# Three read-backs of expert gates move from the sync queue to GpSimd's queue

## What is computed

```python
def _L1_ffn_ref(x, router_w, router_b, expert_w, expert_b):
    scores = jnp.einsum('bsh,eh->bse', x, router_w) + router_b
    probs = jax.nn.softmax(scores, axis=-1)
    top_probs, expert_ids = jax.lax.top_k(probs, K)
    y = jnp.einsum('bsh,edh->bsed', x, expert_w) + expert_b
    out_k = jnp.take_along_axis(y, expert_ids[..., None], axis=2)
    w = top_probs / (jnp.sum(top_probs, axis=-1, keepdims=True) + 1e-09)
    out = jnp.einsum('bsk,bskh->bsh', w, out_k)
    return out
```

## Time and profile before

| what | value |
|---|---|
| median of 3 runs | 945.74 us (945.5 to 946.44) |
| the profiled execution | 946.11 us |
| its span, from the first to the last instruction | 944.3 us |
| busy in the span: PE, DVE, ACT, POOL | 741.0, 576.6, 404.1, 386.8 us |

### The profile page before, as it was taken

How to read it: one execution, slowest core, us unless ns; L and a number is a source line. 1 busy time by engine, 2 the same in 40 slices (tenths; PEclk the granted TensorE clock), 3 DMA queues, 4 the chain that set the end, 5 groups by cost and what they waited for, 6 DMA issues and landing times. The chain is left out here.

```text
span 944.3 us, 11558 instructions
## 1 busy us (share of the span) xinstructions
PE 741.0 (78%) x3622; PEld 585.7 (62%) x3622; DVE 576.6 (61%) x994; ACT 404.1 (43%) x875; POOL 386.8 (41%) x305
## 2 busy tenths in 40 slices
PE   7877888685547869877999677888886997787688
PEld 5645656454327869877898545666664775565455
DVE  4167779679765532312111387899796859777835
ACT  1549275374233324422245373644724455355120
POOL 1045745655672411303003144654366433653430
PEclk9899999798677989999999888888977999899899
DMA  9469755355494658888677597787679565967600
GB/s 353 128 205 343 228 154 152 91 136 142 127 266 113 185 170 242 254 258 232 191 241 223 152 233 190 195 220 189 158 201 252 151 168 143 268 167 187 195 1 21
DMA packets 84067, 177.66 MB, mean 188 GB/s; under 512 B 12671, under 2 KB 32357, under 8 KB 83365
## 3 DMA queue, kind: packets, MB, share of 16 engines
q1 hardware_dynamic: 79172, 169.67, 63.6%
q0 software_dynamic: 4832, 7.24, 2.6%
HBM read 156.15 MB, written 20.69 MB: 187 GB/s over the span
## 5 line engine op out<-in xcount | busy, mean ns | idle before, releaser
L1759 PE MATMUL PS<-PR,CM 128*128 128x304 f32 (+1 forms) x672 | 186.8, 420 | 92.3 <-POOL PR L806 63.2
L806 POOL TENSOR_TENSOR PR<-ST,V 128x608 f32<-128x608 f32 x96 | 142.4, 1483 | 185.5 <-DVE ST L1340 153.8
L1759 PEld LDWEIGHTS PS<-PR,CM 128*128 128x128 f32 x672 | 126.8, 221 | 134.7 <-POOL PR L806 76.8
L976 ACT ACTIVATE dA<-dA,negA 128x304 f32<-128x304 f32 x192 | 93.7, 540 | 151.3 <-DMA BB<-rows_d 151.1
L1340 DVE TENSOR_TENSOR_SCAN ST<-dA,PS 128x608 f32<-128x608 f32 x96 | 136.4, 1420 | 15.1 <-ACT dA L976 11.0
L1028 ACT ACTIVATE HID<-PS,WX 128x128 f32<-128x128 f32 x204 | 59.6, 367 | 150.0 <-PE PS L1759 149.9
L719 POOL TENSOR_TENSOR dA<-dA,aP 128x607 f32<-128x607 f32 x48 | 70.7, 1474 | 71.5 <-ACT aP L996 69.7
L1536 DVE TENSOR_TENSOR xp<-PS,WXB 128x192 f32<-128x192 f32 x34 | 12.2, 358 | 127.0 <-PE PS L1759 127.0
L1329 DVE TENSOR_TENSOR PS<-BB,PS 128x608 f32<-128x608 f32 x96 | 76.2, 794 | 21.5 <-DMA BB<-rows_d 10.7
L1759 PE MATMUL PS<-XT,WX 128*128 128x128 f32 x408 | 83.3, 288 | 1.0 <-ACT HID L1028 1.0
L1759 PE MATMUL PS<-XT,WXR 128*128 128x128 f32 x408 | 83.0, 287 | 0.0
(11 more groups left out here) (380 smaller groups left out, 1318.6 us busy)
## 6 DMA issues: line engine op xcount, KB each, us to landing
dA<-rows_d SPq DMA_DIRECT2D x144, 304.0 KB, 4.4
BB<-rows_d SPq DMA_DIRECT2D x144, 304.0 KB, 5.1
WX<-ex_m SPq DMA_DIRECT2D x34, 576.0 KB, 4.0
WX<-ex_m SPq DMA_DIRECT2D x34, 387.0 KB, 3.8
slots_d<-WXR SPq DMA_DIRECT2D x8, 960.0 KB, 8.8
WXR<-ex_r SPq DMA_DIRECT2D x34, 192.0 KB, 4.9
CM<-c SPq DMA_DIRECT2D x1, 4430.0 KB, 19.6
WX<-gates_d SPq DMA_DIRECT2D x3, 1216.0 KB, 6.6
```

The source lines that it names most:

```text
L806: nc.gpsimd.tensor_tensor(PRq[:, c % 2], STq[:, c % 2], DIRS[k].Cw.unsqueeze(1).broadcast_to([128, QB, T]), ALU.mult).then_inc(q_product.s ...
L976: last = nc.scalar.activation(dAq[:, slot, i, :], dAq[:, slot, i, :], ACT.Exp, scale=negA[:, j:j + 1])
L1759: return nc.tensor.matmul(out, lhsT, rhs, start=first, stop=last)
```

## The change

The body of `read_gates` is the same, but it stands on POOL's queue instead of SP's. In `part_b`, POOL calls it ahead of its eleventh product (n = 10). `write_gates` stays on SP.

```diff
@@ SP
-            def read_gates(g):
-
-                sp.wait_ge(gates_out.sem, gates_out.after(g, 16))
-                sp.dma_start(GX[:, 0:EXPERTS, :].rearrange("p e t -> p (e t)"),
-                             gates_d.rearrange("e t -> (e t)").unsqueeze(0).broadcast_to([128, EXPERTS * T])).then_inc(gates_in.sem, 16)
-                for h in range(2):
-                    every = gates_d.rearrange("(e h) t -> h e t", h=2)[h:h + 1, :, :]
-                    sp.dma_start(GX[h * DR:(h + 1) * DR, EXPERTS:, :], every.broadcast_to([DR, EXPERTS // 2, T])).then_inc(gates_in.sem, 16)
...
                 if g + 1 < GROUPS:
                     write_rows(g + 1, 0)
-                if g:
-                    read_gates(g - 1)
             store(GROUPS - 2)
@@ POOL
+            def read_gates(g):
+
+                pool.wait_ge(gates_out.sem, gates_out.after(g, 16))
+                pool.dma_start(GX[:, 0:EXPERTS, :].rearrange("p e t -> p (e t)"),
+                             gates_d.rearrange("e t -> (e t)").unsqueeze(0).broadcast_to([128, EXPERTS * T])).then_inc(gates_in.sem, 16)
+                for h in range(2):
+                    every = gates_d.rearrange("(e h) t -> h e t", h=2)[h:h + 1, :, :]
+                    pool.dma_start(GX[h * DR:(h + 1) * DR, EXPERTS:, :], every.broadcast_to([DR, EXPERTS // 2, T])).then_inc(gates_in.sem, 16)
...
             def part_b(g, tail, nxt):
                 far = after_next(nxt)
                 for n in range(QSTEPS):
+                    if g is not None and tail is not None and n == 10:
+                        read_gates(tail)
                     if g is not None:
                         product_step(g, 1, n)
```

## The result

The changed kernel takes 958.88 us (median of 4 runs, 955.56 to 960.67) where the kernel before took 945.7 us beside it: 13.2 us between the medians. The ratio of runs taken side by side is 1.0106, 95% interval 1.0073 to 1.0140, so 10 us slower (7 to 13). The forecast was 950.1 us, its range ended at 953.0.

What follows compares the result with a forecast made beforehand. No engine holds the span; the last-ending waits at the three gate reads count, with DMA engines full at the seams. 946.11 + 1.8 (end) + 2.6 (seams) = 950.5, or 950.1 us on the median's scale; range 944.8 to 953.0.

Steps and rivals of the forecast that it cites:

- The last read: End of program: POOL issues the gate read 1.6 us later than SP, first byte 0.2 us later; +1.8 us.
- the two delayed products: End: POOL's last two products, delayed up to 3.5 us by the three issues, finish before the first mixture piece.
- The late start of the seams: Both seams: row reads wait for the last row write to land, so the first transfer comes 1.3 us later.
- If the DMA engines do the same 11.6 us of work from a start 1.3 us later, the last of what PE needs lands 1.3 us later: Both seams: full engines move 3040 KB at an unchanged rate; +1.3 us at each, +2.6 us.
- The slow clock behind a waiting PE: Seams: idle PE restarts at the 1.2 GHz level; only a rival counted it, up to 2.5 us of work lost.
- the rival with a cold PE: Seams: all four slots get ahead of the gates, and PE's slow stretch begins later; 951.3 us, chance 0.15.
- PE needs all 3040 KB before it can run on: Seams: PE's step 1 order needs the gates (1824 KB) and two row slots (608 KB each).
- Gates last: Seams: four slots get ahead, gates in at 819.7 us at the second; 5.6 us in all, 951.3 us, chance 0.15.
- the 0.4 us for landing: Second seam, gates-last case: added to the transfers' end at 819.3 us, putting the gates at 819.7 us.
- The seams cancel: Seams: engines alternate between queues, second slot 1 us earlier, gates 0.9 us late; seams cost about 0; 947.5 us, chance 0.20.
- The marks: Signs for right: DVE's first seam wait gone or short, a later wait instead; POOL's last pieces at about 899.3 us.
- The mark against it: Seams: DMA windows well over 269 GB/s would make the forecast fall, since it rests on full engines.

Runs made afterwards that it cites:

- The second set: The changed kernel itself, timed again beside the kernel before: ratio 1.0083 (1.0050 to 1.0117), or 7.9 us slower.
- e1: Kernel before with only the last gate read on POOL's queue (n = 10), the seams still on SP: ratio 1.0046 (1.0016 to 1.0075).
- e5: Kernel before with the seam gate reads on ACT's queue, behind POOL's tenth backward product; last read on SP: ratio 1.0025 (0.9998 to 1.0053).
- e11: Changed kernel with ACT's output instructions ahead of the exponentials of steps 2 to 4: ratio 1.0123 (1.0085 to 1.0161).
- e6: Kernel before, but at the seams SP issues the gate reads behind the second slot's row reads: ratio 1.0053 (1.0023 to 1.0083).
- e2: Kernel before with only the seam gate reads on POOL's queue (n = 10), the last read on SP: ratio 1.0066 (1.0038 to 1.0094).
- e3: Changed kernel, but SP asks for the third slot's rows only once the gates have landed: ratio 1.0134 (1.0083 to 1.0186).
- e14: e3 with ACT's output instructions ahead of the exponentials of steps 2 to 4, at the two seams with gates only: ratio 1.0103 (1.0071 to 1.0135).
- e4: Kernel before with the seam gate reads on POOL's queue one product earlier (n = 9), last read on SP: ratio 1.0015 (0.9979 to 1.0051).
- e9: e6 with ACT's output instructions ahead of the exponentials of steps 2 to 4, also where no gates are read: ratio 1.0062 (1.0025 to 1.0098).

## Why the prediction was wrong

The direction was right, the size not: 10 us by the ratio, 13.2 between the medians, against a forecast of 4.4 (a ratio of 1.0047). The second set, 1.0083 (1.0050 to 1.0117), is nearer, but does not reach down to the forecast either. By its steps:

- *The last read: right, with one term left out.* "+1.8 us" stands against 10.73 - 8.83 = 1.9 us from POOL's tenth product to the first piece. That the two delayed products are hidden was right too. Left out were 1.4 us behind the first piece, 48.3 us to the end instead of 46.9: the eight matmuls behind YS ran at a clock of 0.63 and took 3.56 us instead of 2.31. The late read alone does not explain that clock (last section). The end cost 3.3 us; e1 measures 0.0046, some 4 us (1.5 to 7).
- *The late start of the seams: right as a start.* The row reads are issued 1.96 us behind the last row write, where gates were issued 0.64 us behind it; 1.3 us. By the packet records the first packet came 1.45 us later (3.30 instead of 1.85 us behind that write). No run has this late start alone, so its price by itself was not measured.
- *"If the DMA engines do the same 11.6 us of work from a start 1.3 us later, the last of what PE needs lands 1.3 us later": the step that failed.* At the first seam the second slot came 1.0 us later, and 0.5 us of it was left at the next seam. At the second seam it came 4.0 us later, and the gates were used 3.5 us later. The engines were full, as argued, but neither the work nor its rate was the same. From the first packet to DVE's product of step 1 it was, already before, 13.08 us and not 11.6, at 268 GB/s, 3.51 MB, and 15.63 us at 241 GB/s after, 3.77 MB (3040 KB are 3.11 MB). An estimate from these rows splits the 4.0 us: 1.45 are the later start, about 1.6 the lower rate, and about 1.0 the rows of the third and fourth slots, more of which went ahead of the last of the second. The rows of the second slot, which used to follow the gates on one queue, now took turns with them and got a quarter of the bytes while both were moving (the counts beside e5).
- *The slow clock behind a waiting PE: put at nothing in the forecast.* The output projection starts 3.8 us later behind the row write, but part 0 of the mixture ends 5.1 us later. The 1.3 us between are PE's clock: it was 0.50 from 825.5 to 830.7 us, the 1.2 GHz level, and part 0 took 2.18 us instead of 1.19. Before, the slow stretch of the earlier trace rows had begun with the sum of step 0, ahead of the projection. Only the rival with a cold PE had priced this.
- *"PE needs all 3040 KB before it can run on": true of the changed kernel, incomplete as a rule.* There PE waited for the second slot (10.2 us for DVE HID), and e11 shows that ACT was not what it waited for. But e6 shows a third claim right behind it, the fifth step's rows through ACT's order, which the working left out.
- *The rivals.* "Gates last" put the gates at 819.7 us, 19.5 us behind the row write; POOL's first piece began 19.8 us behind it (the 0.4 us for landing, which had no row, were 1.0: the last packet ended 18.8 us behind it). The gates did come last, but the price of 5.6 us was too low: the rival left the second slot on time, and that came late as well. "The seams cancel" had the turns right, which the packet counts show, but it took the rate as undiminished, the small gate pieces as half a row's size (from POOL's queue they were packets of twice that size), and the third and fourth slots as staying behind the second. From that it had the second slot 1 us earlier, and it came 4 us later. The range left no room for both coming late together.
- *The marks.* Those named for a right forecast came true: DVE's first wait was 0.22 us, its second 9.7, and POOL's last pieces began at 888.62 + 10.73 = 899.35 us on the old scale. They tell which wait ends last, not how long it is. The mark against it, windows well over 269 GB/s, was met in a short window (336 from 812 to 814 us), as it was before the change (326 from 804 to 806); a rate below 269 over the whole block, which is what happened, was no mark at all.

Not settled: why the engines move less while busy. It is low with POOL's queue in this mix (e2, too, moved 207 to 234 GB/s from 812 to 816 us) and not with ACT's. But e6, on SP's queue alone, shows 211 and 229 GB/s from 813 to 817 us, so it is not shown to come from POOL's queue or from two queues. That the third and fourth slots' share costs 1.0 us is read from the bytes; the held runs e3 and e14 could not confirm it, since two records of one program differ by as much.

## What to carry to other kernels

Where the DMA engines are full, the order on one queue is a schedule: moving a transfer to another queue gives that order up. The engines then took turns packet by packet here, the stream with the smaller packets fell behind, and both ended late. Before betting on which bytes a seam needs, walk down every in-order engine behind the transfers; here two short ACT instructions stood behind three exponentials that each waited for rows. And a transfer that is alone on the path (the end) should be issued by whichever engine is idle when its source is ready, the queue itself being worth only some tenths of a microsecond.

## What the runs showed of the hardware

The same 5.6 MB of gates left a different number of packets by queue. The queue lines of the page (packets, MB, share), before:

```profile
q1 hardware_dynamic: 79172, 169.67, 63.6%
q0 software_dynamic: 4832, 7.24, 2.6%
```

and after:

```profile
q1 hardware_dynamic: 77108, 164.07, 60.9%
q0 software_dynamic: 5744, 12.84, 4.7%
```

SP's queue lost 2064 packets, POOL's gained 912: 2.7 KB a packet from SP, 6.1 KB from POOL on average. All of the difference lies in the transfers of 304 KB, 1216 bytes a packet from SP and 4864 from POOL. While both queues had work the engines took nearly as many packets from one as from the other: 208 and 225 in the changed kernel, 458 and 463 in e5. The Trainium skill (DMA: Bandwidth & Descriptors, Queues, rings and completion order) says that each engine goes round the queues packet by packet; these counts agree. So the gates got three quarters of the bytes from POOL's queue, and a third from ACT's while its small packets were moving.

Nor was the size of the clock's part expected: at the second seam 1.3 us, at the end 1.4. The first followed PE's wait of 10.2 us. The second is only in part tied to the late read: from POOL's first piece to the end it is 48.2 to 48.4 us in six of the seven records with the last read at POOL's eleventh product (46.9 in e14), but 48.2 to 48.3 also in e4, e5 and e9, where SP issued it in time, and 46.8 to 46.9 in the rest.
